# Perceiver block on one core: the transposes of gate times up written as products with the identity, and the mix in two groups of 64 tokens

## The reference, cut to what matters

```
x = x + xattn(layernorm(x), ctx)      # attention over the context
x = x + attn(layernorm(x), ...)       # two long convolutions
x = x + ffn(layernorm(x), ...)        # soft mixture of experts: 16 experts, 64 slots each
```

```
slots = einsum('bnd,bnes->besd', x, dispatch)             # 1024 slots = 16 experts x 64
gate  = gelu(einsum('besd,edf->besf', slots, Wg) + bg)    # 64 slots x 512 for each expert
up    = einsum('besd,edf->besf', slots, Wu) + bu
eout  = einsum('besf,efo->beso', gate * up, Wd) + bd      # 64 slots x 256
out   = einsum('bns,bso->bno', combine, eout)             # sum over all 1024 slots
```

## Time and profile before

| | |
|---|---|
| median of 3 runs | 198.26 us (197.84 to 198.4) |
| time of the profiled execution | 198.39 us |
| its span | 196.3 us |
| granted TensorE clock | 0.999 of full speed |
| TensorE busy | 187.9 us, 96% of the span |
| VectorE, ScalarE, GpSimd busy | 126.2, 104.9, 82.3 us |
| HBM read | 46.73 MB, 239 GB/s over the span |

### The profile page before, as it was taken

One profiled execution on the slowest core, in us unless ns is written; L12 is line 12 of the kernel. 1 busy time (PEld: TensorE's weight loads), 2 busy tenths in 40 slices (PEclk: granted clock), 3 DMA queues, 4 the chain that ended last, 5 costly groups with the idle time before them and its releaser, 6 DMA issues.

```text
span 196.3 us, 3858 instructions
## 1 busy us (share of the span) xinstructions
PE 187.9 (96%) x1221; PEld 143.3 (73%) x1221; DVE 126.2 (64%) x268; ACT 104.9 (53%) x215; POOL 82.3 (42%) x61
## 2 busy tenths in 40 slices
PE   7997999999999999999999988999999999999993
PEld 5975999999999999999999976774543644454451
DVE  2656997698778778777877678844563513453431
ACT  1586876786777767768767330267458521122210
POOL 2269998867878768887676022010000000000000
PEclk9999999999999999999999999999999999999999
DMA  5999957866775884984592599999999999853200
GB/s 149 261 367 356 323 159 249 271 214 211 224 231 167 269 273 123 341 238 140 161 232 63 166 360 393 350 384 362 383 366 371 302 335 288 195 137 85 56 0 27
DMA packets 24907, 47.01 MB, mean 239 GB/s; under 512 B 1600, under 2 KB 11968, under 8 KB 24896
## 3 DMA queue, kind: packets, MB, share of 16 engines
q1 hardware_dynamic: 23664, 43.52, 69.1%
q10 hardware_dynamic: 1232, 3.35, 6.8%
HBM read 46.73 MB, written 0.13 MB: 239 GB/s over the span
## 4 chain that ended last, share of the span: by engine, by line
PE 81%; DMA 7%; issue 5%; DVE 3%; SPq 1%; POOL 1%; ACT 1%; POOLq 0%; DVEq 0%
PE bank L638 15%; PE bank L400 10%; PE bank L652 7%; PE bank L441 6%; PE bank L445 6%; PE bank L443 6%; PE bank L413 5%; PE bank L417 5%; PE bank L415 5%; PE bank L426 5%; DMA raw<-in_ctx_dram 5%; PE bank L662 2%; PE bank L669 2%; PE bank L544 2%; DMA W_sb<-in_L_xattn_W_dram 1%
## 5 line engine op out<-in xcount | busy, mean ns | idle before, releaser
L923 POOL TENSOR_TENSOR c_lo<-raw,c_hi 128x1024 fp32r<-128x1024 f32 (+1 forms) x25 | 53.9, 2157 | 21.4 <-ACT c_hi L756 21.1
L1006 DVE TENSOR_TENSOR cT_lo<-bank,cT_hi 128x512 fp32r<-128x512 f32 (+1 forms) x50 | 31.6, 674 | 9.8 <-ACT cT_hi L748 8.8
L748 ACT ACTIVATE cT_hi<-bank 128x512 fp32r<-128x512 f32 (+1 forms) x48 | 25.6, 585 | 9.3 <-PE bank L400 9.3
L441 PE MATMUL bank<-c_hi,pT_hi 128*128 128x258 f32 x98 | 29.9, 305 | 0.0
L445 PE MATMUL bank<-c_hi,pT_lo 128*128 128x258 f32 x98 | 27.7, 283 | 0.0
L443 PE MATMUL bank<-c_lo,pT_hi 128*128 128x256 f32 x98 | 27.6, 281 | 0.0
L400 PE MATMUL bank<-tab,raw 128*128 128x128 f32 x196 | 25.6, 273 | 1.3 <-DMA raw<-in_ctx_dram 1.3
L918 POOL TENSOR_TENSOR c_hi<-raw,zero 128x512 fp32r<-128x512 f32 (+1 forms) x25 | 25.7, 1026 | 2.3 <-DMA raw<-in_ctx_dram 2.3
L400 PEld LDWEIGHTS bank<-tab,raw 128*128 128x128 f32 x196 | 22.0, 141 | 1.7 <-DMA raw<-in_ctx_dram 1.5
L763 ACT ACTIVATE pT_hi<-bank 128x512 fp32r<-128x512 f32 (+1 forms) x25 | 14.8, 590 | 15.0 <-PE bank L426 14.8
L413 PE MATMUL bank<-cT_hi,q_hi 128*128 128x512 f32 (+1 forms) x50 | 21.5, 430 | 0.3 <-DVE q_lo L1055 0.3
(11 more groups left out here) (162 smaller groups left out, 294.4 us busy)
## 6 DMA issues: line engine op xcount, KB each, us to landing
raw<-in_ctx_dram SPq DMA_DIRECT2D x24, 512.0 KB, 3.8
bias<-biases_dram ACTq DMA_DIRECT2D x10, 320.0 KB, 5.7
late_gu<-in_L_ffn_Wg_dram SPq DMA_DIRECT2D x3, 1024.0 KB, 10.8
late_gu<-in_L_ffn_Wu_dram SPq DMA_DIRECT2D x3, 1024.0 KB, 11.6
late_d<-in_L_ffn_Wd_dram SPq DMA_DIRECT2D x3, 1024.0 KB, 13.6
early_gu<-in_L_ffn_Wg_dram SPq DMA_DIRECT2D x4, 512.0 KB, 4.7
early_gu<-in_L_ffn_Wu_dram SPq DMA_DIRECT2D x4, 512.0 KB, 5.0
early_d<-in_L_ffn_Wd_dram SPq DMA_DIRECT2D x4, 512.0 KB, 4.9
```

Of the source, the lines that this page charges most:

```text
L441: nc.tensor.matmul(bank[6 + r][:, 0:D + 2], ph, c_hi[:, slot, t, :], start=(t == 0), stop=False)
L748: nc.scalar.activation(cT_hi[:, g % 2, h, 0:n], bank[h][:, 0:n], ACT.Copy).then_inc(cThi_rdy, 1)
L923: nc.gpsimd.tensor_tensor(c_lo[:, slot, 0:nt, :], raw[:, slot, 0:nt, :], c_hi[:, slot, 0:nt, 0:D].bitcast(fp32), ALU.subtract).then_inc(cl ...
L1006: nc.vector.tensor_tensor(cT_lo[:, g % 2, h, 0:n], bank[h][:, 0:n], cT_hi[:, g % 2, h, 0:n].bitcast(fp32), ALU.subtract).then_inc(cTlo_rdy, 1)
```

## The change

The four wide transposes of `hid` become eight narrow matmuls with the identity as the moving operand, each transposing 64 slots x 128 columns. The one wide mix matmul becomes two narrow ones, 64 tokens each. Nothing else differs: waits, semaphores, banks and the order of the steps stay.

```
             def hidden_transpose(p):
                 pe.wait_ge(hid_rdy, p + 1)
                 if p >= 1:
                     pe.wait_ge(hidT_rdy, p)
                 for c in range(FC):
-                    last = nc.tensor.transpose(bank[3][:, c * P:(c + 1) * P], hid[:, c * P:(c + 1) * P], ident)
+                    for a in range(2):
+                        last = nc.tensor.matmul(bank[3][a * SL:(a + 1) * SL, c * P:(c + 1) * P],
+                                                hid[:, c * P + a * SL:c * P + (a + 1) * SL], ident,
+                                                start=True, stop=True)
                 last.then_inc(hidT_ps, 1)
 
             def mix_of(p):
...
-                last = nc.tensor.matmul(bank[1][:, 0:D], combT[:, p, :], eout[:, p % 2, :],
-                                        start=(p == 0), stop=(p == PAIRS - 1))
+                for a in range(2):
+                    last = nc.tensor.matmul(bank[1][a * SL:(a + 1) * SL, 0:D],
+                                            combT[:, p, a * SL:(a + 1) * SL], eout[:, p % 2, :],
+                                            start=(p == 0), stop=(p == PAIRS - 1))
                 last.then_inc(mix_ps, 1)
```

## The result

The changed kernel takes 198.96 us (median of 13 runs, 198.62 to 199.63), the kernel before 197.97 us in the same 13 rounds (197.24 to 198.4). The ratio is 1.0057, 95% interval 1.0042 to 1.0071: slower by 1.1 us (0.99 us between the two medians). Forecast were +1.3 us and 199.6 us.

The account below looks back on a forecast made before the run. TensorE alone was taken to bound the kernel; +0.31 (pair 0), +0.81 (pairs 2 to 7) and +0.19 (closing step) make +1.31 on 198.39, 199.7, less 0.13 for the median: 199.6 us, range 198.7 to 200.6.

Parts of the forecast that it names:

- The slot of the narrow product: Transposes: two paired narrow instructions with 128 moving columns take 0.109 us; eight slots 0.87, +0.436 us each call.
- The upper bounds: Narrow transposes: 0.14 us a slot if loads cannot overlap, 201.6 us; or 0.108 a matmul, 206.5 us.
- the density rival: Narrow transposes held to 0.06 us a matmul, 200.3 us; chance 0.07 for 0.06 to 0.14, 0.03 for 0.108.
- The mix at no cost: Mix: two narrow products pair up and take 0.43 us as the wide one did; bound +0.43 each.
- The excursions: TensorE going from narrow to wide and back costs 0.30 us extra; six go away, in pairs 2 to 7.
- Pair 0: Its transposes follow wide line 580, so the width change moves ahead of them: 4.36 us for 4.07, +0.31.
- Pairs 2 to 7: Each: transposes +0.436 less 0.30 for the excursion, net +0.135; six times +0.81 us.
- The closing step: Last steps: transposes +0.436 on the path, less 0.09, 0.11 and 0.05 around the mixes: +0.19 us.
- The cover: Up (1.72 us) covers ScalarE's later `hidT` copy except in the closing step; `hid` of pair 4 adds no wait.
- The landing of the bias: Pair 4: bias DMAs issue 0.7 us later, as TensorE does; only a landing slipping by more adds a wait.
- The four times of the Trainium skill: Transpose mode four times faster for fp32: a call 1.74 us, the whole 206.7; the prediction read two times from the trace.

Follow-up runs that it names:

- both orders: Kernel before, with mix 5 behind the transposes of pair 7, mix 6 behind down 7, transposes of pair 1 behind up of pair 2: 199.00 us, ratio 1.0051.
- the four wide products: Kernel before, with the transposes as four wide fp32 products with the identity, the mix wide as before: 201.99 us, ratio 1.0197.

## Why the prediction was right

*What bounds the kernel.* TensorE alone set the end of pairs 2 to 7. Eight kernels that add, take or move its work come out within 0.04 us of their sums, read by the distance. The ninth, with both orders, missed by 2.35 us, because there other engines were late.

*The slot of the narrow product.* I took 0.109 us from half of down's slot. The transposes take 0.87 to 0.88 us for eight such slots, 0.109 each, or 0.054 for each MATMUL. The upper bounds (0.14 for a slot whose load can't overlap, 0.108 for a matmul) are refuted: one load row holds 14 loads in 0.80 us. With them falls the density rival.

*The mix at no cost.* Its own work is 0.43 us before and after.

*The excursions.* They cost 0.30 us by subtraction of four gaps, and 0.41 less 0.109 when one is added by itself. Six are gone, one has moved, as counted in the order. Pair 0 came to 4.36 us as worked out, with the start 0.03 later, +0.32 for a forecast of +0.31. Pairs 2 to 7 were to give +0.81 and gave +0.77: 0.13 each as forecast, but 0.11 in pair 2, where the routing's work takes 0.03 us less.

*The closing step.* It was to give +0.19 and gave +0.20; the sum of the whole left 0.02 over.

*The cover.* `hid` of pair 4 was ready at 170.91 and its transposes started at 171.60 with no wait; TensorE was 0.59 us late there, where 0.7 had been worked out. The landing of the bias was the term I could not bound well. ScalarE issued its DMAs 0.72 us later after line 580 than before (19.13 for 18.41), as forecast, but VectorE took the bias up at the same time, 28.3 us after it in both kernels. Nothing in the working said that it would not slip; that it didn't is in part luck. In the kernel with both orders it slipped.

*The four times of the Trainium skill* ("TensorE: Matmul & The Clock Gate", section Terms) are not what these runs show at 128 moving columns. Against 0.43 us for the four wide transposes, the four wide products take 0.89 and the eight narrow ones 0.87, twice as much. A narrow transpose was not run.

*What was off.* 199.6 us was forecast and 198.96 measured. Some 0.3 us of this is the base, 197.97 in the longer series instead of the 198.26 that I added to. The rest is the rise, 1.31 against the 0.99 between the medians. The ratio of the runs gives 1.13, with an interval from 0.83 to 1.41 that takes in the forecast, and the distance 1.29.

## What to carry to other kernels

Count changes of array width along TensorE's order and give each pair of them a price. Here it was 0.30 us where a transpose is the first wide instruction and 0.35 where a wide product is, however much stood in between. Then compare it with what the work in between costs in the other form. The mix costs the same at either width, so making it narrow is free. The transposes give up a cheaper mode, 0.44 us a call, which is more than the excursion of 0.30 that it removes, and so the kernel is slower. Before moving a step to save such a gap, look at which engine's copy hangs on it and what that engine does next.

## What the runs showed that I had not expected

TensorE kept up 32 instructions (16 matmuls, 16 loads) in 0.87 us, four times the loads and matmuls of the wide transposes in twice the time, and a slot still took 0.109 us as the moving columns alone would have it. No denser run was tried. And the stages ahead of the change, equal in all kernels, varied by 1.3 us between single profiled executions, as much as the change itself.
